# First attention layer of a two-layer graph network: the W2 products are issued behind the second source tile of a chunk's sums instead of ahead of the first

## What is computed

```python
h = (x @ W).reshape(N, H, C)
e = jax.nn.leaky_relu(al_s[src] + al_d[dst], NEG_SLOPE)
m = jax.ops.segment_max(e, dst, num_segments=N)
ex = jnp.exp(e - m[dst])
denom = jax.ops.segment_sum(ex, dst, num_segments=N)
alpha = ex / (denom[dst] + 1e-16)
out = jax.ops.segment_sum(h[src] * alpha[:, :, None], dst, num_segments=N)
...
h = jax.nn.elu(_gat_layer(x, src, dst, W1, att_src1, att_dst1, b1, concat=True))
out = _gat_layer(h, src, dst, W2, att_src2, att_dst2, b2, concat=False)
```

## Time and profile before

| | |
|---|---|
| median of 3 runs | 1311.3 us (1308.69 to 1316.64) |
| span of the profiled execution | 1313.7 us |
| PE busy | 1179.4 us, 90% |
| DVE busy | 911.6 us, 69% |
| ACT busy | 500.1 us, 38% |
| the 20 chunks of the first layer | from 329.7 to about 844 us of the span |
| L1207, sums of the first layer | 2400 products |
| L1235, W2 products | 960 products |

### The profile page before, as it was taken

One profiled execution on the slowest core, in us unless ns is written; L12 is line 12 of the kernel. 1 busy time (PEld: TensorE's weight loads), 2 busy tenths in 40 slices (PEclk: granted clock), 3 DMA queues, 4 the chain that ended last, 5 costly groups with the idle time before them and its releaser, 6 DMA issues. The chain is left out here.

```text
span 1313.7 us, 21059 instructions
## 1 busy us (share of the span) xinstructions
PE 1179.4 (90%) x7582; PEld 1093.7 (83%) x7582; DVE 911.6 (69%) x1939; ACT 500.1 (38%) x1109; POOL 49.5 (4%) x46
## 2 busy tenths in 40 slices
PE   2799998999799999999999999848997899979998
PEld 2576776867798999899989999838997799979998
DVE  7797888984987688768876687579766733363321
ACT  1313131222665556554655566135532311142110
POOL 7000000000100000000000000000002300000000
PEclk9799999999999999999999999978998999989999
DMA  5022033100200200020102000003001200050001
GB/s 191 17 56 83 36 102 95 44 9 0 81 25 1 81 23 27 1 81 13 37 1 81 16 34 1 0 13 118 1 1 61 79 31 26 25 187 25 31 31 34
DMA packets 28410, 59.09 MB, mean 45 GB/s; under 512 B 2883, under 2 KB 8043, under 8 KB 28305
## 3 DMA queue, kind: packets, MB, share of 16 engines
q1 hardware_dynamic: 28112, 57.35, 13.3%
q10 hardware_dynamic: 192, 0.32, 0.1%
HBM read 42.12 MB, written 15.54 MB: 44 GB/s over the span
## 5 line engine op out<-in xcount | busy, mean ns | idle before, releaser
L1207 PE MATMUL banks<-hs,ring_hi 128*128 128x258 f32 (+1 forms) x1600 | 300.4, 288 | 4.0 <-DVE ring_lo L474 2.1
L1207 PEld LDWEIGHTS banks<-hs,ring_hi 128*128 128x128 f32 (+1 forms) x1600 | 248.8, 189 | 5.7 <-issue 2.5
L1207 PE MATMUL banks<-hs,ring_lo 128*128 128x258 f32 (+1 forms) x800 | 227.1, 284 | 0.0
L1699 PE MATMUL p_y<-cr_hi,g_hi 128*128 128x256 f32 (+1 forms) x600 | 148.2, 289 | 19.5 <-ACT cr_hi L1558 15.5
L448 ACT ACTIVATE e<-banks,al 128x256 f32<-128x256 f32 (+1 forms) x400 | 155.8, 492 | 16.4 <-PE banks L433 16.4
L1207 PEld LDWEIGHTS banks<-hs,ring_lo 128*128 128x128 f32 (+1 forms) x800 | 151.2, 189 | 0.0
L1699 PE MATMUL p_y<-cr_hi,g_lo 128*128 128x256 f32 (+1 forms) x600 | 147.0, 286 | 0.0
L456 ACT ACTIVATE ring_hi<-pf 128x512 fp32r<-128x512 f32 (+1 forms) x125 | 81.5, 652 | 158.7 <-DVE pf L467 154.0
L1699 PEld LDWEIGHTS p_y<-cr_hi,g_hi 128*128 128x128 f32 x600 | 118.7, 198 | 21.2 <-ACT cr_hi L1558 21.2
L1235 PE MATMUL banks<-w_hi,oT_hi 128*128 128x384 f32 (+1 forms) x320 | 111.1, 347 | 12.6 <-DVE rows L949 6.9
L1699 PEld LDWEIGHTS p_y<-cr_hi,g_lo 128*128 128x128 f32 x600 | 118.8, 198 | 0.0
(11 more groups left out here) (221 smaller groups left out, 2127.9 us busy)
## 6 DMA issues: line engine op xcount, KB each, us to landing
h_scratch<-stage SPq DMA_DIRECT2D x30, 256.0 KB, 2.0
hs<-h_scratch SPq DMA_DIRECT2D x30, 256.0 KB, 2.9
w_st<-in_L_gnn_W SPq DMA_DIRECT2D x4, 1536.0 KB, 10.4
w_st<-in_L_gnn_W SPq DMA_DIRECT2D x16, 384.0 KB, 3.4
gw_st<-in_L_gnn_W SPq DMA_DIRECT2D x12, 384.0 KB, 3.3
xr<-in_x SPq DMA_DIRECT2D x9, 384.0 KB, 6.4
rows<-in_x SPq DMA_DIRECT2D x9, 384.0 KB, 3.6
g_scratch<-orow SPq DMA_DIRECT2D x18, 192.0 KB
```

Source lines behind the costliest of these rows:

```text
L1207: last = nc.tensor.matmul(p_a[0:m, dt, half, 0:HH], wt.ring[a][:, s // G, s % G, dt * P:dt * P + m], hs[:, s, b, half * HH:(half + 1) * HH ...
L1699: last = nc.tensor.matmul(p_y[:, f, 0:n], hs[a][:, s, f * P:(f + 1) * P], c_hi[:, i % RS, s % G, 0:n], start=s + a == 0, stop=s == T - 1 a ...
```

## The change

The call of `products(q - 2)` leaves the loop over the chunks and goes into `sums(q)`, behind source tile 1. It stands there behind the broadcast for the next chunk, which is issued at the same tile, and ahead of `turn_next` and `turn_out`. No instruction is added or removed, and the programs of the other four engines are the same. The two last calls, `products(18)` and `products(19)` behind the loop, stay.

```diff
--- before
+++ after
@@ -1214,6 +1214,8 @@
                     if s == 2 * G - 1 and c == NC - 1 and not final:
                         pe.wait_ge(shift_out, h + 2)
                         wt.broadcast(nc, pe, pick, shiftT[:, h + 1, :], q + 1, 0)
+                    if s == 1 and before(q, 2) is not None:
+                        products(before(q, 2))
                     if c == NC - 2 and not final:
                         turn_next(h, s)
                     if q >= 1 and s in TURNS:
@@ -1238,8 +1240,6 @@
                     last.then_inc(g_ready, 1)
 
             for q in range(HEADS * NC):
-                if before(q, 2) is not None:
-                    products(before(q, 2))
                 sums(q)
             products(HEADS * NC - 2)
             for dt in range(NDT):
```

## The result

| | before | after |
|---|---|---|
| median | 1310.1 us (1308.7 to 1316.6, 4 runs) | 1445.0 us (1443.6 to 1446.2, 4 runs) |
| span of the profiled execution | 1313.7 us | 1444.6 us |
| first layer, first to last sums | 329.7 to 843.7: 514.0 us | 330.7 to 973.6: 642.9 us |
| ahead of it / behind it | 329.7 / 470.0 us | 330.7 / 471.0 us |
| pauses of PE over 0.15 us in the layer | 27.3 us in 17 | 114.9 us in 40 |

The changed kernel takes 1.100 times as long (95% interval 1.097 to 1.103). The forecast was 1437 us, range 1402 to 1462. Nearly all of it, 128.9 of 130.9 us between the two profiled executions, lies in the first layer. Its length is counted from the start of its first sums to the start of the products behind its last ones.

A forecast was written before the change was run, and what follows sets the result against it. The prediction took TensorE's own program as the bound. Border waits of 57.5 us, turn waits of 34.8 and 33 for the clock made 125 us, on 1311.3 us a forecast of 1437 us, range 1402 to 1462.

The forecast's parts named there:

- Term 1: At the chunk borders, a chunk's sums wait for VectorE's z, about 3.5 us at most borders; 57.5 us in all.
- Term 2: Within the sums, turn 0 waits for the ELU, and turn 1 too in the last head; 34.8 us in all.
- Term 3: Behind the longer pauses TensorE's clock falls to half: 23 more slow stretches at 1.45 us each, 33 us.
- some of the slow stretch lies in the pause itself, so 1.45 us each and not 1.63: In the clock's share: each slow stretch behind a pause costs 1.45 us, less than the 1.63 us read at 454.77.
- The rule of the Trainium skill: The clock falls to half only after at least one whole idle window of its monitor; without the 33 us.
- No cost in clock: Rival: the pauses come as summed, 92 us, and TensorE's clock holds; 1403 us, chance 8%.
- Short pauses: Rival: each border costs only 1.83 us as at chunk 1, the turns nothing; 1329 up to 1345 us, chance 6%.
- It feeds itself: Rival: a late elu_out delays the next z, each chunk adding 1 to 2 us more; 1457 to 1472 us, chance 10%.
- Not slower: Rival: the earlier broadcast lets ScalarE run ahead, z is ready at the border; 15 us less, 1296 us, chance 1%.
- Pauses of 3.1 us and more I take to cost it always: In the clock's share: every TensorE pause of 3.1 us or more brings the low clock, 18 at the borders.

The follow-up runs named there:

- e_turns35: The changed kernel with turn 1 behind source tile 5 and not 6; 1428.7 us.
- e_wait_first: The kernel before, products still ahead of the sums, but TensorE waits for z_done already ahead of the products; 1418.8 us.
- e_halves: Against the kernel before, parts 0 and 1 of the products stay ahead of the sums, parts 2 and 3 go behind source tile 1; 1356.5 us.
- e_tile0: The changed kernel with the products behind source tile 0 of a chunk's sums and not 1; 1420.0 us.
- the two bases: The kernel before with asserted bounds on the edge-window words, 1325.5 us, and with a mask on them instead, 1314.6 us.
- e_filler: The changed kernel with throw-away products (18; 30 at c = 0, 15 at c = 4) ahead of the wait for z at each border; 1422.7 us.
- c_light: The kernel before with each edge-window word masked to 31 bits, one register operation an engine; 1314.6 us.

## Why the prediction was right, step by step

**The bound.** TensorE's program is the bound of the stage, and its pauses add to the time. In the changed kernel the layer is 128.9 us longer, VectorE's and ScalarE's work the same.

**Term 1, 57.5 us.** The border waits came as read from the timeline of before: forecast 3.52 us start to start, measured 3.36 to 3.38 us of idle time (3.26 behind c = 0) with 0.16 us of overlap; at c = 0 5.58 of idle time against 5.77, at c = 4 2.97 to 2.99 us where 1.50 stood (+1.48), at q = 19 2.93. In sum 65.3 us of new waits, less 4.5 and 5.5 that went, and 12 x 0.16: 57.2 us. That turn 1 sets them, but at c = 4, is shown by e_turns35, that the early broadcast changes nothing by e_wait_first, which has the late one and the same waits.

**Term 2, 34.8 us.** The turns' waits went from 8.5 to 40.9 us; with the overlap at eleven more of them 34.1. By kind: 2.12 to 2.28 us at c = 0 and 2 (2.2 to 2.6 forecast), 4.97 at c = 1 (5.04), 3.56 in the last head (3.6), 0.07 at c = 4 (0.2), turn 1 in the last head 1.62, 2.33 and 5.01 (1.8, 2.5, 5.2). The term at c = 0 was the only one that rested on a choice between two bounds (14.0 us from the products to `elu_out`, between 13.6 and 15.2; measured 13.8), and is the one that is off, by 0.3 us of idle time. The terms of the last head add up to 8.95 us and not 8.8, which changes nothing. e_halves shows that this wait hangs on the last part of the products and not on the late borders, e_tile0 that it is the distance from there to turn 0, broadcast included, set against VectorE's work up to `elu_out`.

**Term 3, 33 us.** What is left of the 128.9 us is 37.6. Its size was low by about 5 us, but that it came so near is in part luck: two errors nearly cancel. The count was too high. 23 more slow stretches were forecast, the profile has 17 more: one behind 17 of the 18 borders (the pause of 2.99 us at chunk 4 kept the clock) and three at turn 0 of c = 1, less the three of before that went. None of the six waits of 2.1 to 2.3 us at turn 0 was followed by the low clock, where four were counted, and the last head has no further one (the one behind turn 1 of chunk 19 was there before, and is now twice as long). The cost of one was too low: 37.6 / 17 = 2.2 us and not 1.45. The step that fell short is "some of the slow stretch lies in the pause itself, so 1.45 us each and not 1.63": where the clock fell well within the pause, the slow stretch was twice as long as the ones seen before, see below. The rule of the Trainium skill (TensorE: Matmul & The Clock Gate, Part 1), as the prediction tells it, does not hold here: the clock fell behind pauses of 1.83 us in the kernel before, and with that rule the sum would have been 1403 us, 42 below the measured time.

**The sum.** 125 us were forecast on the median; it moved by 134.9 us. Between the two profiled executions it is 130.9 us: 4.6 of the missing 5.9 are term 3, 2.0 lie outside the layer (ahead and behind, 1.0 each, not forecast), and -0.7 terms 1 and 2. The other 4.0 us are the starting point: the profiled execution of before has its span 3.6 us above the median of before as it is now known, and its layer is 1.5 and 4.2 us longer than that of the two bases, with more of the low clock.

**The rivals.** No cost in clock: excluded by e_filler. Short pauses: excluded by the waits themselves, 3.4 and not 1.83 us. It feeds itself: the ELU ends 13.8 us behind the start of the products at c = 2 in the first and the third head alike, and the border behind the longest wait of a turn is 3.37 us like the others. Not slower: the chain from turned tile 1 to `z` kept its 7.62 us.

## What to carry to other kernels

A block of work that waits for nothing, standing between two that share a buffer, may be the only cover of that buffer's emptying. Before moving it, read how late the emptying ends against the block's start, and not only whether anyone waits today; here that one subtraction (3.5 us at most of the 18 borders) gave 57 of the 129 us, and most of the clock's share came on top of it. Then count what stands behind the moved block on the other engines and where the mover meets it again: the same move took 3.6 us from the distance between the products and turn 0. Splitting the block gives the cover back, and that was most of the loss (1356.5 us for 1445.0), but it does not help the second wait if the last part ends where it ended after the move.

## What the runs showed of the hardware

Most pauses of 3.4 us cost more than their length. Windows of the changed kernel across the starts of chunk 2 (first three rows) and chunk 3 (last three); the clock is the last but two columns:

```profile
371.80:375.00 3.20, 0.00 (x0) 0.00 (x0) 3.13 (x7) 2.08 (x6) 0.00 (x0) 0.89 0.00 0
375.10:377.70 2.60, 2.60 (x12) 2.60 (x13) 0.00 (x0) 2.09 (x4) 0.00 (x0) 0.50 0.00 0
377.80:380.50 2.70, 2.70 (x14) 2.47 (x13) 0.00 (x0) 0.00 (x0) 0.00 (x0) 0.50 0.03 6
405.00:408.30 3.30, 0.00 (x0) 0.00 (x0) 3.25 (x7) 2.19 (x6) 0.00 (x0) 1.00 0.00 0
408.50:411.70 3.20, 3.20 (x16) 3.20 (x17) 0.00 (x0) 2.01 (x4) 0.00 (x0) 0.50 0.00 0
412.00:415.00 3.00, 3.00 (x21) 2.79 (x20) 0.00 (x0) 0.00 (x0) 0.00 (x0) 1.00 0.00 0
```

Both pauses are 3.4 us long. At chunk 2 the clock fell to 0.5 (1.2 GHz) while TensorE still paused (0.89 in the mean over the pause), and stayed there for all of the first two source tiles; at chunk 3 it fell as the work began, and was back at 1.00 (2.4 GHz) by 412. The two source tiles up to the broadcast, start to start:

```profile
375.02 0.58 PE L1207 MATMUL banks<-hs,ring_hi 128*128 128x258 f32 x1 [3.36 <-DVE z L921]
...
380.48 0.47 PE L433 MATMUL banks<-shiftT,pick 40*128 40x128 f32 x1
...
408.34 0.51 PE L1207 MATMUL banks<-hs,ring_hi 128*128 128x258 f32 x1 [3.37 <-DVE z L921]
...
412.92 0.43 PE L433 MATMUL banks<-shiftT,pick 40*128 40x128 f32 x2
```

5.46 us at chunk 2, 4.58 at chunk 3, and 2.99 without a pause (643.83 in the earlier trace rows to the broadcast at 646.82). So the same pause costs 2.5 or 1.6 us on top of itself, as the fall of the clock comes ahead of its end or at its end. I had taken 1.63 as the most that one pause can cost. In the changed kernel the clock fell 0.7 us or more ahead of the end of the pause at the seven borders that cost 2.3 us and more, and at most 0.4 us ahead of it, or behind it, at the ten that cost 1.3 to 1.6 (the costs as in e_filler).

It can also cost nothing. In e_wait_first the clock stayed at 1.00 behind a border pause of the same 3.37 us, at chunk 13 (a row of the timeline and one of the windows view):

```profile
731.52 0.44 PE L1235 MATMUL banks<-w_hi,oT_hi 128*128 128x384 f32 x1 [3.37 <-DVE z L921]
...
731.60:735.00 3.40, 3.40 (x20) 3.40 (x21) 0.56 (x1) 2.10 (x4) 0.00 (x0) 1.00 0.02 5
```

So the step "Pauses of 3.1 us and more I take to cost it always" of the prediction does not hold either. What decides between the three cases is not shown by these runs.

Also not expected: waits of 1.83 us at c = 0 were followed by the low clock three times out of three in the profile of before, and once out of three in that of c_light, with the same instructions around them. The six new waits of 2.1 to 2.3 us at turn 0 of the changed kernel were followed by it not once; in e_halves, where the same six take 2.1 to 2.3 us, two of them were. A term for such short pauses can only be given as a range.
